# A two-block graph network: the attention mask's self loops as integers on GpSimd, the mask itself by ScalarE's relu, in place of two VectorE instructions per group

## What is computed

```python
mask = adjacency_matrix.astype(jnp.float32) + jnp.eye(n) > 0     # edges and self loops
for l in range(3):
    si, sj = x @ attn_w[l, :d], x @ attn_w[l, d:]
    scores = si[:, :, None] + sj[:, None, :] + attn_b[l]
    scores = jnp.where(scores >= 0, scores, 0.2 * scores)
    attn = softmax(jnp.where(mask, scores, -jnp.inf))
    h = layernorm(x + attn @ x, g1[l], beta1[l])
    x = layernorm(h + gelu(h @ W1[l] + b1[l]) @ W2[l] + b2[l], g2[l], beta2[l])
```

## Time and profile before

| what | value |
|---|---|
| time, median of 3 runs (lowest to highest) | 1514.67 us (1514.05 to 1514.86) |
| the profiled execution, its own time | 1514.97 us |
| its span in the profile | 1513.2 us |
| PE busy | 1464.8 us, 97% of the span |
| DVE, ACT, POOL busy | 90%, 77%, 60% of the span |
| mean granted TensorE clock | 0.988 of full speed |
| share of the chain that ended last | PE 93%, DVE 4% |

### The profile page before, as it was taken

The page is one execution under the profiler, slowest core; times in us unless marked ns, Lnnn a source line. Parts: engine busy times, 40 slices in busy tenths (PEclk is TensorE's granted clock), DMA queues, the critical chain, the costliest instruction groups (busy, mean ns, idle before and its releaser), DMA issues.

```text
span 1513.2 us, 35107 instructions
## 1 busy us (share of the span) xinstructions
PE 1464.8 (97%) x11264; PEld 1242.7 (82%) x11264; DVE 1366.1 (90%) x4311; ACT 1161.8 (77%) x2042; POOL 904.2 (60%) x1006
## 2 busy tenths in 40 slices
PE   6899999499999999999999999999999999999997
PEld 3677777388888888888888888888888888888886
DVE  7999999898989899989898999898989998989864
ACT  5788888468787878787777777777777777777784
POOL 5799998336364647564645566545555665555465
PEclk9999999699999999999999999999999999999999
DMA  6543433610000112110011121100011220000001
GB/s 200 153 153 125 136 126 115 175 38 15 8 15 24 34 35 78 48 32 8 15 26 32 39 74 51 28 8 15 26 32 49 64 64 15 9 15 8 15 29 56
DMA packets 70891, 82.78 MB, mean 55 GB/s; under 512 B 29281, under 2 KB 54113, under 8 KB 70753
## 3 DMA queue, kind: packets, MB, share of 16 engines
q1 hardware_dynamic: 69120, 74.76, 17.0%
q0 software_dynamic: 816, 3.15, 0.6%
q10 hardware_dynamic: 816, 3.15, 0.5%
HBM read 38.95 MB, written 25.17 MB: 42 GB/s over the span
## 4 chain that ended last, share of the span: by engine, by line
PE 93%; DVE 4%; issue 1%; POOL 0%; DMA 0%; ACT 0%; SPq 0%; DVEq 0%; ACTq 0%; POOLq 0%
PE bank L765 36%; PE bank L789 36%; PE bank L357 3%; PE bank L746 3%; PE bank L347 3%; PE bank L755 3%; PE bank L315 2%; PE bank L345 2%; PE bank L332 2%; PE bank L325 1%; PE bank L342 1%; PE bank L734 1%; DVE w_lo L575 0%; PE bank L726 0%; DVE shifted L552 0%
## 5 line engine op out<-in xcount | busy, mean ns | idle before, releaser
L789 PE MATMUL bank<-w_hi,hid_hi 128*128 128x256 f32 x1528 | 428.1, 280 | 1.3 <-DVE hid_lo L1028 1.3
L789 PE MATMUL bank<-w_hi,hid_lo 128*128 128x256 f32 x1528 | 427.2, 280 | 0.0
L789 PE MATMUL bank<-w_lo,hid_hi 128*128 128x256 f32 x1528 | 426.7, 279 | 0.0
L844 ACT ACTIVATE bank<-bank,b_col 128x512 f32<-128x512 f32 x384 | 251.8, 656 | 196.1 <-PE bank L765 195.2
L765 PE MATMUL bank<-nT_hi,w_hi 128*128 128x512 f32 x768 | 317.3, 413 | 1.6 <-DVE nT_lo L1157 1.6
L1028 DVE TENSOR_TENSOR hid_lo<-bank,hid_hi 128x512 fp32r<-128x512 f32 x384 | 259.5, 683 | 60.7 <-ACT hid_hi L849 58.8
L765 PE MATMUL bank<-nT_hi,w_lo 128*128 128x512 f32 x768 | 304.6, 397 | 0.0
L765 PE MATMUL bank<-nT_lo,w_hi 128*128 128x512 f32 x768 | 304.0, 396 | 0.0
L789 PEld LDWEIGHTS bank<-w_hi,hid_hi 128*128 128x128 f32 x1528 | 286.7, 188 | 15.2 <-DVE hid_lo L1028 1.7
L789 PEld LDWEIGHTS bank<-w_lo,hid_hi 128*128 128x128 f32 x1528 | 286.3, 187 | 13.1
L789 PEld LDWEIGHTS bank<-w_hi,hid_lo 128*128 128x128 f32 x1528 | 287.1, 188 | 0.0
(11 more groups left out here) (137 smaller groups left out, 3127.3 us busy)
## 6 DMA issues: line engine op xcount, KB each, us to landing
raw_weights<-xin SPq DMA_DIRECT2D x96, 128.0 KB, 2.3
xin<-in_x_dram SPq DMA_DIRECT2D x16, 512.0 KB, 4.0
first_block_out<-x_res SPq DMA_DIRECT2D x16, 512.0 KB, 2.7
second_block_in<-x_act SPq DMA_DIRECT2D x16, 512.0 KB, 3.7
xin<-second_block_in SPq DMA_DIRECT2D x16, 512.0 KB, 3.9
x_fin<-first_block_out SPq DMA_DIRECT2D x16, 512.0 KB, 4.0
out_dram<-x_fin SPq DMA_DIRECT2D x15, 512.0 KB, 2.9
xh_other<-xh SPq DMA_DIRECT2D x128, 33.0 KB, 2.1
```

Of the source, the lines that this page charges most:

```text
L789: mm = pe.matmul(FF[t // 2][:, (t % 2) * D:(t % 2 + 1) * D], a[:, r, t * P:(t + 1) * P], w[:, l, c, :], start=(c == 0 and t % 2 == 0 and p ...
L844: act.activation(h[:], h[:], ACT.Gelu, bias=b1_col[:, l, c:c + 1]).then_inc(s_gelu, 1)
```

## The change

`adj_raw` now gets the self loops in place: GpSimd adds the integer one-hot rows `node_int` (`add_loops`). ScalarE then computes the mask as relu(-1e30 * a + 1e30), which is 1e30 where the sum `a` is 0 and 0 where it is 1 or more (`make_mask`, now in its program), and `scores` subtracts it. VectorE has no mask work any more; its count of steps per slot falls from 9 to 7, and the `sem_inc` that stood for the two steps in layers 1 and 2 goes too. Two constants are made at the start by VectorE: `far` (1e30 in one column) and `node_int` (a cast of `node_of`).

```diff
+                dve.memset(far[:], -NEG).then_inc(q_loops, 1)
+                dve.tensor_copy(node_int[:], node_of[:]).then_inc(q_loops, 1)
...
             def second_scalar(act):
+                def make_mask(i, s):
+                    l, g = layer_group(s)
+                    V = i * SLOTS + s
+                    act.wait_ge(s_edges, V // SLOTS * QG + g + 1)
+                    at_least(act, s_sc, 7 * (V - QG + 1))
+                    act.activation(mask[:, g].rearrange("p t j -> p (t j)"), adj_raw[:, g].rearrange("p t j -> p (t j)"),
+                                   ACT.Relu, bias=far[:], scale=NEG).then_inc(s_mask, 1)
...
                 def tail(tau):
+                    if tau == NT + 4:
+                        act.wait_ge(q_loops, 2)
+                        make_mask(0, 0)
                     if tau == NT + 7:
                         exp(0, 0)
                     if tau == NT + 8:
                         keep_attn(0, 0)
+                        make_mask(0, 1)
...
                             high(U, s, c)
+                            if nxt2 and c == 1 and layer_group(s + 2)[0] == 0:
+                                make_mask(i, s + 2)
...
             def second_gpsimd(pool):
+                def add_loops(i, s):
+                    l, g = layer_group(s)
+                    V = i * SLOTS + s
+                    pool.wait_ge(s_in[g], 32 * (V // SLOTS + 1))
+                    pool.tensor_tensor(adj_raw[:, g], adj_raw[:, g], node_int[:].unsqueeze(1).broadcast_to([P, TG, N]),
+                                       ALU.add).then_inc(s_edges, 1)
...
                             post(i, s - 1)
+                        if nxt3 and layer_group(s + 3)[0] == 0:
+                            add_loops(i, s + 3)
+
+                def tail(tau):
+                    if tau == NT + 2:
+                        pool.wait_ge(q_loops, 2)
+                        add_loops(0, 0)
+                    if tau == NT + 5:
+                        add_loops(0, 1)
+                    if tau == NT + 8:
+                        add_loops(0, 2)
...
             def second_vector(dve):
-                score = Steps(dve, s_sc, 9)
+                score = Steps(dve, s_sc, 7)
...
-                def make_mask(i, s):
-                    if l == 0:
-                        dve.wait_ge(s_in[g], 32 * (i + s // SLOTS + 1))
-                        score.done(dve.tensor_tensor(mask_sum, adj_raw[:, g], node_of[:].unsqueeze(1).broadcast_to([P, TG, N]),
-                                                     ALU.add))
-                        score.wait()
-                        score.done(dve.tensor_scalar(mask[:, g], mask_sum, 0.0, NEG, ALU.is_le, ALU.mult))
-                        score.wait()
-                    else:
-                        score.k += 2
-                        dve.sem_inc(s_sc, 2)
...
+                    if l == 0:
+                        dve.wait_ge(s_mask, (V // SLOTS * QG + g + 1))
                     dve.wait_ge(s_spread, V + 1)
...
-                                                            mask[:, g, t, :], ALU.add, ALU.add))
+                                                            mask[:, g, t, :], ALU.add, ALU.subtract))
```

More of the change, by code:

```diff
@@ L102, in graph_net @@
         same_graph = sb("same_graph", [P, P])
+        node_int = sb("node_int", [P, N], I32)
+        far = sb("far", [P, 1])
         minus_half = sb("minus_half", [P, TG])
@@ L137, in graph_net @@
         diag_hi, diag_lo = (sb(n, [P, TG, N], F32R) for n in ("diag_hi", "diag_lo"))
-        mask_sum = in_raw(2048, TG, N)
         scored2, leaky2, shifted2 = (in_raw(at, TG, N) for at in (2560, 2816, 3072))
@@ L189, in graph_net @@
             q_st = sem("first_stored")
-            q_zero = sem("first_filled")
+            q_zero, q_loops = sem("first_filled"), sem("self_loops_made")
             q_mv, q_rs, q_nmr, q_h = sem("q_mean_var"), sem("q_rstd"), sem("q_shift"), sem("q_h")
@@ L607, in graph_net @@
             s_nT, s_nhi, s_nlo, s_base = sem("nT"), sem("nT_hi_ready"), sem("nT_lo_ready"), sem("base_ready")
+            s_edges, s_mask = sem("edges_with_loops"), sem("mask_made")
             s_nfull = sem("nT_scaled")
@@ L1017, in after @@
                         pool.tensor_tensor(nm_f[:, half], ng_f[:, half], rs_f[:, half], ALU.mult).then_inc(e_nm, 1)
-                first_gpsimd(pool, lambda tau: None)
+                first_gpsimd(pool, tail)
                 slots(pool, before, some, after)
             def second_vector(dve):
-                score = Steps(dve, s_sc, 9)
+                score = Steps(dve, s_sc, 7)
                 def low(U, s, c):
@@ L1072, in dots_of, with diagonal @@
                                                      ALU.mult, ALU.add, dst[:, t:t + 1]).then_inc(s_dots, 1)
-                def make_mask(i, s):
+                def diagonal(i, s):
                     l, g = layer_group(s)
@@ L1077, in make_mask @@
                     score.unit(V)
-                    if l == 0:
-                        dve.wait_ge(s_in[g], 32 * (i + s // SLOTS + 1))
-                        score.done(dve.tensor_tensor(mask_sum, adj_raw[:, g], node_of[:].unsqueeze(1).broadcast_to([P, TG, N]),
-                                                     ALU.add))
-                        score.wait()
-                        score.done(dve.tensor_scalar(mask[:, g], mask_sum, 0.0, NEG, ALU.is_le, ALU.mult))
-                        score.wait()
-                    else:
-                        score.k += 2
-                        dve.sem_inc(s_sc, 2)
-                def diagonal(i, s):
-                    l, g = layer_group(s)
-                    V = i * SLOTS + s
                     dve.wait_ge(s_dots, 2 * TG * (V + 1))
@@ L1105, in scores @@
                     V = i * SLOTS + s
-                    score.resume(V, 3)
+                    score.resume(V, 1)
                     score.wait()
+                    if l == 0:
+                        dve.wait_ge(s_mask, (V // SLOTS * QG + g + 1))
                     dve.wait_ge(s_spread, V + 1)
@@ L1162, in tail @@
                         dve.tensor_copy(same_graph_r[:], same_graph[:]).then_inc(s_samer, 1)
-                    if tau == NT + 3:
+                    if tau == NT + 4:
                         dve.wait_ge(s_w2lo, NT - HEAD)
-                        make_mask(0, 0)
-                    if tau == NT + 4:
                         dve.wait_ge(s_rows, 16 * 3)
@@ L1174, in tail @@
                     if tau == NT + 7:
-                        make_mask(0, 1)
                         dots_of(0, 1, range(0, 2))
@@ L1208, in some @@
                         low(U, s, 1)
-                        if U == 0:
-                            make_mask(0, 2)
                         if nxt:
@@ L1226, in some @@
                             scores(0, 2)
-                        if nxt3:
-                            make_mask(i, s + 3)
                         low(U, s, 5)
```

## The result

The changed kernel takes 1516.51 us (median of 20 runs, 1515.68 to 1518.69) against 1514.32 for the kernel before beside it (20 runs, 1513.03 to 1515.73). The ratio is 1.0016, with a 95% interval from 1.0009 to 1.0022: slower by 2.2 us, where I had forecast 1.65 us less. That is still within the 0.2% that I had called "same", but the sign is wrong and the time is outside my range.

What follows compares the result with a forecast made beforehand. PE was taken to bound the kernel, so only its waits for VectorE counted: 1514.97 - 0.45 (hand-over) - 1.2 (first slot) = 1513.3 us, a median of about 1513.0, called "same"; range 1511.4 to 1514.3.

Steps and rivals of the forecast that it cites:

- GpSimd's adds in slots (13): Ahead of `make_base` in the slots: adds of 0.7 to 0.9 us hidden by GpSimd's 8.4 us waits, cost nothing.
- My bound on the price: GpSimd's add in the slots: only beyond some 4 us would it make `make_base` late, thirteen times.
- the first rival: Hand-over and first slot: a new wait eats part of the gain or the stall moves, 1513.2 to 1513.9 us; chance 0.20.
- Group 0's mask and add in the hand-over: Hand-over: removing VectorE's mask gains 0.54 us, the rest becoming a wait for `scored`; GpSimd's add costs nothing below 0.80 us.
- my sum of 0.55 and 0.25 us of slack: Hand-over: GpSimd idle 0.55 us ahead of `rstd`, `x_res` 0.25 early for VectorE, so an add costs from 0.80 us.
- Group 1's and 2's adds: Hand-over: they fall where GpSimd waits for VectorE's next variance, so cost nothing; cover gone, 0.7 to 0.9 us each.
- the 0.54 by which I had the first `hidden` earlier: Start of the first slot: matmuls begin 0.54 us earlier, at 299.25; 0.45 of it taken as gain because of the clock.
- Group 3's mask: First slot: removing it from VectorE ends PE's 1.29 us stall ahead of `output(5)`; less 0.1 at `low(7)`, gain 1.2 us.
- ScalarE's masks: Behind `high(1)` in the slots: 0.5 us each, hidden in ScalarE's waits for PE, with no table load.
- The removed masks in slots give nothing: Slots where PE never waits: taking mask instructions off VectorE, such as group 2's behind `low(1)`, gains nothing.
- The dear add: GpSimd's integer add is slow: at 3.5 us each 1515.7 us, at 5 some 1530; chance 0.05.
- The clock's rival: First slot: PE's clock returns sooner, down to about 1510.3 us, chance 0.12; 3 us later leaves 1514.4.

Runs made afterwards that it cites:

- The experiments behind `take_y`: GpSimd's slot add placed behind VectorE's `take_y`: in the changed kernel 1513.33 us, with a second, unread add 1513.63; an unread add in the kernel before 1514.19.
- the last experiment: The kernel before, with only group 3's mask in the first slot moved within VectorE, behind `low` of block 7 and `split_n`: 1513.74 us.

## Why the prediction was wrong, by its steps

*"GpSimd's adds in slots (13) stand ahead of make_base, behind which GpSimd waits 385.5 us in 46 places, 8.4 each, for VectorE. An add of 0.7 to 0.9 there is hidden."* This is the step that failed; it was worth 3.8 us, not 0. The wait is real and is still there. It says that nobody waits for a result of GpSimd in that stretch, but not that nobody waits for GpSimd to stop. However long the wait, it could not hide an add placed ahead of it, because VectorE's third dot gets on only when GpSimd's last instruction ends. The experiments behind `take_y` show it from both kernels. My bound on the price, "beyond some 4 us it would make `make_base` late in the slots", was wrong by the same step: the slack was 0.28 us. The Trainium skill (SBUF — State Buffer, "Who interferes with whom"), which I had cited for the first rival (there miscounted as the second), has the rule: a VectorE instruction with two SBUF inputs and a GpSimd instruction that reads SBUF exclude each other for a whole instruction. The traces agree, in that held dots end 0.28 to 0.29 us behind the GpSimd instruction in all five cases read. They show that VectorE is held and until when; that it is a port that holds it no run here isolates. I had used that rule for the first slot and the hand-over, not for the thirteen places where the change put GpSimd work.

*Group 0's mask and add in the hand-over*: the mask's part was about right, the add's "I take nothing" was short by 0.13 us. L522 or L525, the `stats` of step `NT + 4`, starts 5.28 us behind the `x_res` at 263.38 before, 4.69 behind the same `x_res` (263.77) without adds, and 4.82 (263.66) in the changed kernel. `leaky` waits 0.20 us for `scored`, where I had said some 0.5, and 0.58 without adds. The add took 0.73, within the 0.69 to 0.87 that I had bounded, but one thing was missed: VectorE's `neg`, an instruction on 128x2 numbers, took 0.50 us beside this add where it took 0.12 a step earlier. It stands ahead of `vare`, for which GpSimd's `rstd` waits, so my sum of 0.55 and 0.25 us of slack did not hold. POOL and DVE, then the same DVE instruction without adds:

```profile
265.64 0.73 POOL L990 TENSOR_TENSOR adjin<-adjin,node_int 128x256 int32<-128x256 int32 x1
...
265.90 0.50 DVE L550 TENSOR_SCALAR neg<-mv 128x2 f32<-128x2 f32 x1
...
267.74 0.69 DVE L521 SCALAR_TENSOR_TENSOR leaky<-bank,scored 128x512 f32<-128x512 f32 x1 [0.20 <-ACT scored L405]
```

```profile
266.00 0.12 DVE L550 TENSOR_SCALAR neg<-mv 128x2 f32<-128x2 f32 x1
```

`neg` reads a single tile, so two operands are not needed for a hold: VectorE's second mask instruction, L1083, reads one tile too and took 1.26 to 1.27 us in all 12 slots beside GpSimd, against 0.29 with GpSimd idle in the last experiment.

*"Group 1's and 2's adds ... The add of group 1 comes when GpSimd waits for VectorE's next variance"*: the same mistake as in the slots. GpSimd waits there, and VectorE computes dots; the third took 0.97 instead of 0.42. Counted from `x_res` at 263.38, 263.66, 263.77 and 263.34 to the first residual, the hand-over takes 25.42 us before, 25.65 after, 24.95 without adds and 25.10 with group 1's add moved. So of the 0.54 by which I had the first `hidden` earlier, 0.47 was there as long as no add ate it. The 0.15 between the last two figures is what group 0's add costs: with group 1's moved, `neg` still takes 0.49 and L525 still starts 4.81 behind `x_res`.

*Group 3's mask*: right. The first slot is 1.35 us shorter, where I had taken 1.2, and of the "0 to 0.2" of a new stall at `low(7)` the trace of the changed kernel has 0.2. Its timeline of DVE, and the waits of that slot, answer to the earlier trace rows:

```profile
321.94 0.96 DVE L1142 TENSOR_TENSOR raw_weights<-raw_weights,top 128x256 f32<-128x256 f32 x1
322.82 0.68 DVE L1064 TENSOR_TENSOR hid_lo<-bank,hid_hi 128x512 fp32r<-128x512 f32 x1
```

```profile
PEld bank L793 <- DVE hid_lo L1064: 0.2, 1, 0.2
```

*ScalarE's masks*: right, 0.51 us each and hidden, as the kernel without adds shows. *The removed masks in slots give nothing*: right for PE, and seen in where the time went. Of the 2.17 us that the pair takes in such a slot VectorE now waits 1.41 for ScalarE in slot 12 (0.42 ahead of `nT_lo`, 0.99 ahead of `hid_lo`) and spends 1.04 more in the held dot.

*The rivals.* The first, "a new wait eats the part", named the right mechanism (the port) with the wrong place and so a price of 0.2 to 0.9 us (1513.2 to 1513.9 against 1513.0) instead of 3.8. The dear add named the right instruction, but 0.75 us is not dear; its place was. The clock's rival did not come: the granted clock returned 5.7 us behind the first `hidden` in the changed kernel and 5.9 before, while it scatters by more between executions of kernels that are the same up to there (last section).

What stays open: no run moved group 0's add, so its 0.15 us rests on the traces alone, and the 1513.33 and 1513.63 of the kernels with one and two adds behind `take_y` can't be told apart.

## What to carry to other kernels

On this kernel, an engine's idle time was room only for work that fell into it. Before putting an instruction on GpSimd, look at what VectorE does while it would run, and whether one of VectorE's instructions on SBUF tiles already ends right behind one of GpSimd's; if so, both engines are in one round, and a GpSimd instruction in it costs its whole length once the round is longer than PE's slot. Tie the added instruction to a point where the traces show VectorE's instructions as short beside GpSimd as alone (here `hid_lo`, the statistics and the reduction), by a wait if need be. And measure slots by their starts, since a busy time of 1099.7 of 1100 us hid 3.8 us.

## What was new about the hardware

- A held dot of 128x256 ended at a fixed distance behind GpSimd's instruction: 0.28 us (602.72 + 1.45 against 603.89), 0.29 (578.48 against 578.19), 0.28 (605.78 against 605.50), 0.28 (601.76 against 601.48), and 0.28 in the hand-over (277.97 against 277.69). An unheld dot takes 0.42 in all, so it had waited with most of its work still to do. The held `neg` of 128x2 ended 0.03 behind (266.40 against 266.37).
- An integer add of 128x256 took GpSimd 0.75 us on the mean, and 0.61 with both inputs one 128x64 tile read four times.
- The clock's return at the start of the second part differs from one profiled execution to the next: it came 5.9 us behind the first `hidden` in the kernel before (299.79) and 3.9 in the last experiment (298.72), whose program up to there is the same. From 304 to 308 us the granted clock was 0.78 and 1.00, as the windows of these two show:

```profile
304.00:308.00 4.00, 4.00 (x26) 2.41 (x26) 2.20 (x7) 1.41 (x3) 2.30 (x2) 0.78 0.47 145
```

```profile
304.00:308.00 4.00, 4.00 (x36) 3.24 (x29) 2.87 (x3) 2.28 (x4) 4.00 (x4) 1.00 0.23 76
```

  The slot ahead of the first one takes 22.05 and 21.31 us in them. This alone is 0.7 us between single executions, so it takes the medians, or the slots behind it, to judge an edit of this size.
